# A gated cross-attention and FFN block on Trainium2: the first slots of a software pipeline written out as an opening with its own order, context and Wk/Wv first

## The chip, the cores and the metric

The kernel runs on one core of one Trainium2 chip. Time is device microseconds (us) of one execution, over several executions; the profile is of one execution, taken by the hardware profiler.

## What is computed

A batch `x` of 16 sequences of 256 rows by 512, a context of 16 x 256 x 128. The reference, cut to what matters:

```python
def xattn(q, latent_kv, Wq, Wkv_expand, Wout):      # 16 heads of 32
    qp = q @ Wq.T
    k, v = jnp.split(latent_kv @ Wkv_expand.T, 2, axis=-1)
    scores = jnp.einsum('bhqd,bhkd->bhqk', heads(qp), heads(k)) / jnp.sqrt(32)
    scores = jnp.where(causal, scores, jnp.finfo(scores.dtype).min)
    return merge(softmax(scores) @ heads(v)) @ Wout.T

def ffn(x, w_gate_up, w_down):                      # int8-like quantise and dequantise of
    gate, up = split(qd(x) @ qd(w_gate_up).T)       # rows of x, the weights and h: qd()
    return qd(silu(gate) * up) @ qd(w_down).T

x = x + jnp.tanh(g_xattn[0]) * xattn(layernorm(x), ctx_512, Wq, Wkv_expand, Wout)
x = x + jnp.tanh(g_ffn[0]) * ffn(layernorm(x), w_gate_up, w_down)
```

## The kernel before

Five engines run programs written by hand, in order, and wait for each other on counting semaphores. TensorE (`pe`) multiplies, VectorE (`dve`), ScalarE (`act`) and GpSimd (`pool`) work on tiles, and SyncE (`sp`) issues nearly all DMAs, in order, from one queue.

The attention half is a software pipeline over the 16 batches. `run` calls `slot(b)` for b from -3 to 13, then an ending, then the FFN tiles. In slot b the probabilities of batch b are made and weighed, batch b+1 is scored for its maxima, batch b+2's queries and keys are made and spread, batch b+3 is normalised and transposed, and the outputs of batch b-1 are finished. A step whose batch is not there (`present`) is left out, so slots -3 to 0 are the same list with holes, and slot 1 is the first without any (but for the steps of batches b-2 and b-3, which are on other engines than TensorE).

The steps of one batch X that the texts speak of, in the order in which they depend on each other:

- `load_rows`, `measure_x`, `rsqrt1`, `norm1`: x is loaded to `xln`, its statistics taken (VectorE), the inverse root (GpSimd), normalised (ScalarE).
- `transposed(X, t)`: TensorE transposes `xln` (L1281). `high_t` and `copy_t` (ScalarE) copy it out of PSUM as `xT_hi` and `both`; `low_t` (GpSimd, L537) makes `xT_lo`, their difference. All large products are made of three such products: high by high, low by high, high by low.
- `split_context` (GpSimd, L496 and L498) makes `c_hi`, `c_lo` of the loaded context `craw`; `keys` (L1331) and `values` (L1354) multiply it with Wk and Wv (`wkv_hi`, `wkv_lo`); `queries` (L1344) multiply xT with Wq, 12 products of 128x256 in each of four groups.
- `high_q`, `split_q` (VectorE, L1028), `high_k`, `copy_k`, `low_k` (GpSimd, L545): the same split for q and k.
- `spread_q_hi`, `..._lo`, `spread_k_hi`, `..._lo` (SyncE, L262): four quarters of DMAs of 128 KB each, which lay q and k out by heads in the tile `heads`. Three groups of 32 rows hold hi and lo; two more rows hold the negated maxima against a constant 1 (the memset of `heads`, L1086).
- `scores` (L1295, L1297): one head's scores; `maxima` (VectorE, L995) takes row maxima; `negate`, `maxima_rows` (L1304), `copy_rows` and `move_rows` (the only DMA that ScalarE issues here) put them into `heads`.
- `score_pair` (L1382, L1384): scores of two heads, transposed; `exps` (ScalarE, L775) the exponentials; `select` and `add_blocks` (GpSimd, L522, L530) mask and add; `weigh` (L1408) multiplies with v and sums.
- `weigh_rows`, `weights`, `move_weights`, `load_weights`: the FFN weights are quantised in pieces, one a slot, beside this.

PSUM has eight banks. Two (0, 1) are for scores, two (2, 3) for score pairs, 4 and 5 for weighing and 6 and 7 for everything else, in turn: a table `WORK` says in which order the steps of a slot use the two, and `work_bank` makes each wait until the one before it in that bank has been copied out.

What is done once (the splits of the weights, the tables, the memsets of `heads`) stands in `if b == FIRST` and `if b == FIRST + 1` inside of `slot`.

## Time and profile before

| | us |
|---|---|
| median of 3 runs (lowest to highest) | 771.4 (769.3 to 772.21) |
| the profiled execution | 771.57 |
| its span, first to last instruction | 769.7 |
| busy: TensorE, VectorE, ScalarE, GpSimd | 717.2, 621.4, 412.9, 580.1 |
| mean granted clock of TensorE | 0.971 |

The span is what the trace covers, and times in the trace count from its start. The granted clock is a share of full speed, so 0.50 is the lower of TensorE's two levels (1.2 GHz) and 1.00 the upper (2.4 GHz).

### The profile page before, as it was taken

The numbers are of one execution on the slowest core, as the hardware profiler recorded it, in microseconds if no ns is written. First come the engines' busy times: TensorE is split into PE (matmuls) and PEld (weight loads), VectorE is DVE, ScalarE is ACT, GpSimd is POOL, SyncE is SP. The second block draws the span as 40 slices with busy tenths as digits, with TensorE's granted clock in tenths as the row PEclk, the third lists the DMA queues.
The fourth block names the chain that finished last, engine by engine and source line by source line (L and its number), as shares of the span: only waits on it lengthen the run. The fifth ranks groups of instructions, "written<-read, shape, count | busy, mean of one in ns | idle before, by whom it ended". The sixth has DMA issues, their size and how long they took to land.

```text
span 769.7 us, 17015 instructions
## 1 busy us (share of the span) xinstructions
PE 717.2 (93%) x5345; PEld 515.8 (67%) x5345; DVE 621.4 (81%) x1894; ACT 412.9 (54%) x657; POOL 580.1 (75%) x766
## 2 busy tenths in 40 slices
PE   2488899999999999999999999999999999999993
PEld 2477788798788888888887886755544444444441
DVE  4644867888879789789789878779999999999982
ACT  5433675775765775765765753455534443443440
POOL 5433776887877977977977965668888888888884
PEclk9676999999999999999999999999999999999998
DMA  7685767869769679779779559974846755665665
GB/s 236 154 221 139 203 174 185 203 193 222 199 174 248 169 197 247 174 198 219 201 201 240 141 138 218 244 186 80 162 119 149 160 129 143 153 148 133 146 145 161
DMA packets 137919, 137.59 MB, mean 179 GB/s; under 512 B 90317, under 2 KB 99815, under 8 KB 137703
## 3 DMA queue, kind: packets, MB, share of 16 engines
q1 hardware_dynamic: 136768, 135.97, 71.5%
q8 instruction: 44, 0.72, 0.4%
q10 hardware_dynamic: 1063, 0.54, 0.4%
q14 instruction: 44, 0.36, 0.2%
HBM read 40.24 MB, written 25.31 MB: 85 GB/s over the span
## 4 chain that ended last, share of the span: by engine, by line
PE 60%; issue 13%; POOL 13%; DVE 6%; DMA 5%; ACT 2%; SPq 1%; POOLq 0%; ACTq 0%; DVEq 0%
PE psum L1344 11%; PE psum L1366 10%; PE psum L1408 9%; POOL hidden L664 5%; PE psum L1626 5%; PE psum L1297 5%; PE psum L1382 4%; PE psum L1295 4%; POOL y L678 4%; PE psum L1354 3%; PE psum L1331 3%; DMA x1b<-x_scratch 2%; DMA heads<-nmT 2%; POOL hq L671 2%; PE psum L1636 2%
## 5 line engine op out<-in xcount | busy, mean ns | idle before, releaser
L995 DVE CUSTOM_DVE_ANT_0 junk<-psum,mask 128x128 f32<-128x128 f32 (+1 forms) x512 | 153.7, 353 | 68.9 <-PE psum L1297 66.7
L1626 PE MATMUL psum<-w1q,xqb 128*128 128x512 bf16 (+1 forms) x768 | 158.1, 361 | 1.2 <-DVE u L1036 1.2
L664 POOL TENSOR_TENSOR hidden<-hidden 128x512 f32<-128x512 f32 (+1 forms) x96 | 112.6, 1188 | 28.9 <-ACT hidden L931 28.6
L775 ACT ACTIVATE prob<-psum 128x768 f32<-128x768 f32 x128 | 103.5, 809 | 52.7 <-PE psum L1384 51.4
L1626 PEld LDWEIGHTS psum<-w1q,xqb 128*128 128x128 bf16 x768 | 74.4, 98 | 80.1 <-DVE u L1036 1.6
L936 ACT ACTIVATE hidden<-hidden,round_bias,hinv 128x1408 f32<-128x1408 f32 x32 | 49.9, 1560 | 113.7 <-DVE hinv L1250 113.7
L522 POOL TENSOR_SCALAR_AFFINE_SELECT prob<-prob 128x512 f32<-128x512 f32 x128 | 81.4, 639 | 32.0 <-ACT prob L775 30.9
L530 POOL TENSOR_TENSOR prob<-prob 128x256 f32<-128x256 f32 x128 | 98.1, 772 | 6.5
L1636 PE MATMUL psum<-w2q,hqT 128*128 128x512 bf16 x352 | 82.6, 385 | 6.2 <-DMA hqT<-hq 6.2
L1344 PE MATMUL psum<-xT_hi,wq_hi 128*128 128x256 f32 x256 | 75.8, 296 | 10.0 <-POOL xT_lo L537 10.0
L1297 PE MATMUL psum<-heads 96*128 96x256 f32 x256 | 78.0, 341 | 0.0
L1344 PE MATMUL psum<-xT_hi,wq_lo 128*128 128x256 f32 x256 | 74.6, 291 | 0.0
L1344 PE MATMUL psum<-xT_lo,wq_hi 128*128 128x256 f32 x256 | 74.4, 291 | 0.0
L1382 PE MATMUL psum<-heads 98*128 98x256 f32 x256 | 69.2, 321 | 4.4 <-DMA heads<-nmT 3.9
L1222 DVE SCALAR_TENSOR_TENSOR hidden<-psum,x_scale,s 128x512 f32<-128x512 f32 (+1 forms) x96 | 67.2, 701 | 6.5 <-PE psum L1626 4.2
L1295 PE MATMUL psum<-heads 96*128 96x128 f32 x256 | 69.3, 271 | 3.3 <-DVE mx L995 2.3
L1636 PEld LDWEIGHTS psum<-w2q,hqT 128*128 128x128 bf16 x352 | 34.7, 99 | 46.8 <-issue 9.7
L1232 DVE TENSOR_TENSOR hidden<-psum,s 128x512 f32<-128x512 f32 (+1 forms) x96 | 61.5, 642 | 5.3 <-PE psum L1626 0.2
L1295 PEld LDWEIGHTS psum<-heads 96*128 96x128 f32 x256 | 49.8, 195 | 19.0 <-DVE mx L995 13.7
L1344 PEld LDWEIGHTS psum<-xT_hi,wq_hi 128*128 128x128 f32 x256 | 51.2, 200 | 12.6 <-issue 11.4
L1384 PE MATMUL psum<-heads 98*128 98x128 f32 x256 | 57.4, 224 | 0.0
L931 ACT ACTIVATE hidden<-hidden 128x512 f32<-128x512 f32 (+1 forms) x96 | 50.4, 580 | 11.0 <-DVE hidden L1222 10.9
(116 smaller groups left out, 1798.5 us busy)
## 6 DMA issues: line engine op xcount, KB each, us to landing
heads<-q_hi SPq DMA_DIRECT2D x128, 128.0 KB, 4.3
heads<-k_hi SPq DMA_DIRECT2D x128, 128.0 KB, 4.4
xln<-x_dram SPq DMA_DIRECT2D x16, 512.0 KB, 5.4
heads<-q_lo SPq DMA_DIRECT2D x64, 128.0 KB, 4.0
heads<-k_lo SPq DMA_DIRECT2D x64, 128.0 KB, 3.6
x<-x_dram SPq DMA_DIRECT2D x16, 512.0 KB, 4.2
x_scratch<-x SPq DMA_DIRECT2D x16, 512.0 KB, 4.0
x1b<-x_scratch SPq DMA_DIRECT2D x32, 256.0 KB, 3.4
```

The lines of the kernel that those rows point to most:

```text
L522: pool.affine_select(out=blk, in_=blk, compare_op=ALU.is_ge, fill=0.0, base=0, pattern=[[0, 4], [1, P]], channel_multiplier=-1).then_inc(s ...
L530: pool.tensor_tensor(blk[:, 3], blk[:, 1], blk[:, 2], ALU.add).then_inc(s["added"], 1)
L664: pool.tensor_tensor(up[t % 3][:, o], gate[t % 3][:, o], up[t % 3][:, o], ALU.mult).then_inc(f["prod_done"], 1)
L775: act.activation(prob[:, g % 2, pair % 2, 0:CAUSAL // P].rearrange("p k h q -> p h k q"), psum[:, 2:4, 0:CAUSAL].rearrange("p h (k q) -> p ...
L995: dve.tensor_tensor_reduce(junk[:, n % 2, 0:w], psum[:, h % 2, cols], m, 1.0, LOWEST, ALU.add, ALU.max, mx[:, X % 2, t, h:h + 1]).then_inc ...
L1295: pe.matmul(psum[:, h % 2, 0:P], qs[0:K, X % 2, h, 0:P], ks[0:K, X % 2, h, 0:P], start=True, stop=True)
L1297: pe.matmul(psum[:, h % 2, P:CAUSAL], qs[0:K, X % 2, h, P:S], ks[0:K, X % 2, h, 0:S], start=True, stop=True).then_inc(s["s_done"], 1)
L1344: last = pe.matmul(acc, w[:, k, o], xx[:, k, :], start=(k == n == 0), stop=(k == KH - 1 and n == 2))
L1366: last = pe.matmul(psum[:, bank, :], oo[:, g, o], w[:, g, :], start=(g == n == 0), stop=(g == GROUPS - 1 and n == 2))
L1382: pe.matmul(early, ks[0:K, X % 2, h, 0:P], qs[0:K, X % 2, h, 0:S].rearrange("p (k q) -> p k q", q=P), start=True, stop=True)
L1626: last = pe.matmul(psum[:, bank, 0:w], xqb[:, t % 4, k, :], w1q[:, k, half * I + o:half * I + o + w], start=(k == 0), stop=(k == KH - 1))
L1636: last = pe.matmul(psum[:, 6 + t % 2, :], hqT[:, t % 4, j, :], w2q[:, j, :], start=(j == 0), stop=(j == IT - 1))
```

## The change

`slot(b)` now runs from b = 1, and the steps of slots -3 to 0 are written out in a new function `opening` on each engine, in an order of its own. The same steps are called, each as often as before. SyncE loads the context and Wk/Wv before Wq; Wk/Wv is split first, and the keys and values of batch 0 are multiplied ahead of its queries, in banks 2 to 5, which nothing uses yet. In the opening `work_bank` does not wait; the waits for banks stand in the list itself. The tables of GpSimd are made in two pieces, and the two memsets of `heads` and the tanh of the gates stand at other places.

```diff
-        FIRST = -3
         def work_bank(pe, X, what, t):
 
             at = [w[:2] for w in WORK].index((what, t))
             slot = X - WORK[at][2]
-            if slot >= B - 2:
-                return BANK[what, t]
-            while slot >= FIRST:
+            if slot <= 0 or slot >= B - 2:
+                return bank_of(X, what, t)
+            while True:
...
+        def bank_of(X, what, t):
+
+            first = {("K", 0): 2, ("K", 1): 3, ("V", 0): 4, ("V", 1): 5}
+            return first[what, t] if X == 0 and what in "KV" else BANK[what, t]
...
-        def run(slot, ending, tile):
-
-            for b in range(FIRST, B - 2):
+        def run(opening, slot, ending, tile):
+
+            opening()
+            for b in range(1, B - 2):
                 slot(b)
...
                 sp.dma_start(xln[:], x_tok[0]).then_inc(s["x_loaded"], DMA)
+                sp.dma_start(craw[:], c_bat[0]).then_inc(s["c_loaded"], DMA)
+                sp.dma_start(wkv_raw, WkvT).then_inc(s["wkv_in"], DMA)
                 sp.dma_start(wq_raw, WqT.rearrange("(k p) n -> p k n", p=P)).then_inc(s["wq_in"], DMA)
-                sp.dma_start(wkv_raw, WkvT).then_inc(s["wkv_in"], DMA)
-                sp.dma_start(craw[:], c_bat[0]).then_inc(s["c_loaded"], DMA)
...
+                def opening():
+                    load_rows(1)
+                    spread_k_hi(0, 0)
...
+                def opening():
+                    rsqrt1(0)
+                    split_context(0)
+                    low_t(0, 0)
+                    low_t(0, 1)
+                    low_k(0, 0)
+                    low_k(0, 1)
+                    rsqrt1(1)
...
+                    weights(2)
+                    rsqrt1(3)
+                    split_context(2)
+                    select(0, 0)
...
+                def opening():
+                    high_weights("wkv", wkv_hi, wkv_raw, 1)
+                    norm1(0, 0)
+                    norm1(0, 1)
+                    high_weights("wq", wq_hi, wq_raw, 1)
...
+                    exps(0, 2)
+                    high_k(2, 0)
+                    exps(0, 3)
...
+                def opening():
+                    measure_x(0)
+                    low_weights(0, wkv_hi, wkv_lo, wkv_raw)
+                    low_weights(1, wq_hi, wq_lo, wq_raw)
+                    weigh_rows(0)
+                    measure_x(1)
+                    ones(1)
+                    split_q(0, 0)
+                    split_q(0, 1)
+                    ones(0)
+                    weigh_rows(1)
+                    for h in range(0, 4):
+                        maxima(0, h)
...
+                def opening():
+                    transposed(0, 0)
+                    transposed(0, 1)
+                    keys(0, 0)
+                    keys(0, 1)
+                    values(0, 0)
+                    values(0, 1)
+                    pe.wait_ge(s["t_copied"], 1)
+                    queries(0, 0)
...
+                    pe.wait_ge(s["q_lo"], 1)
+                    transposed(1, 0)
+                    pe.wait_ge(s["q_lo"], 2)
+                    transposed(1, 1)
+                    pe.wait_ge(s["t_copied"], 3)
+                    queries(1, 0)
+                    scores(0, 0)
+                    scores(0, 1)
+                    queries(1, 1)
+                    scores(0, 2)
...
+                    pe.wait_ge(s["t_copied"], 6)
+                    values(1, 0)
+                    maxima_rows(0)
+                    pe.wait_ge(s["t_copied"], 5)
+                    queries(2, 0)
+                    queries(2, 1)
+                    pe.wait_ge(s["v_copied"], 3)
+                    queries(2, 2)
+                    queries(2, 3)
+                    score_pair(0, 0)
+                    pe.wait_ge(s["q_lo"], 5)
+                    values(1, 1)
+                    scores(1, 0)
```

What this does to the engines' programs, at three places. First TensorE's, from its first instruction on. Before, the transposes of batch 0 (`xln`) are followed by the query products (`wq`):

```order
L1281 MATMUL psum<-ident,xln 128x128 x8
L1344 MATMUL psum<-xT_hi,wq_hi 128x256
L1344 MATMUL psum<-xT_hi,wq_lo 128x256
L1344 MATMUL psum<-xT_lo,wq_hi 128x256
L1344 MATMUL psum<-xT_hi,wq_hi 128x256
L1344 MATMUL psum<-xT_hi,wq_lo 128x256
```

Now keys (`wkv`, left out after the first three of twelve) and values (128x512) stand between, and the queries come after them:

```order
L1491 MATMUL psum<-ident,xln 128x128 x8
L1541 MATMUL psum<-c_hi,wkv_hi 128x256
L1541 MATMUL psum<-c_hi,wkv_lo 128x256
L1541 MATMUL psum<-c_lo,wkv_hi 128x256
...
L1564 MATMUL psum<-wkv_hi,c_hi 128x512
L1564 MATMUL psum<-wkv_hi,c_lo 128x512
L1564 MATMUL psum<-wkv_lo,c_hi 128x512
...
L1554 MATMUL psum<-xT_hi,wq_hi 128x256
L1554 MATMUL psum<-xT_hi,wq_lo 128x256
L1554 MATMUL psum<-xT_lo,wq_hi 128x256
```

The 18 products of context and Wk/Wv have moved ahead of the 48 of the queries.

Second, VectorE's program from the first weight split on. Before:

```order
L953 TENSOR_TENSOR wq_lo<-v,wq_hi 128x2048
L1068 TENSOR_REDUCE wmax<-wrow 128x1
L1070 TENSOR_SCALAR w_scale<-wmax 128x1
L1073 RECIPROCAL winv<-w_scale 128x1
L953 TENSOR_TENSOR wkv_lo<-prob,wkv_hi 128x1024
L1086 MEMSET heads 2x4096 x2
L1028 TENSOR_TENSOR q_lo<-psum,q_hi 128x512
L959 BN_STATS st<-xln 128x6 x2
L963 BN_AGGR mv<-st 128x2 x2
L1028 TENSOR_TENSOR q_lo<-psum,q_hi 128x512
L953 TENSOR_TENSOR wo_lo<-prob,wo_hi 128x2048
```

And now (the ISA row is the first of batch 0's maxima; two rows of the weight piece before it are left out):

```order
L1131 TENSOR_TENSOR wkv_lo<-prob,wkv_hi 128x1024
L1131 TENSOR_TENSOR wq_lo<-v,wq_hi 128x2048
L1254 TENSOR_REDUCE wmax<-wrow 128x1
L1256 TENSOR_SCALAR w_scale<-wmax 128x1
L1259 RECIPROCAL winv<-w_scale 128x1
L1145 BN_STATS st<-xln 128x6 x2
L1149 BN_AGGR mv<-st 128x2 x2
L1134 MEMSET heads 2x4096
L1214 TENSOR_TENSOR q_lo<-psum,q_hi 128x512 x2
L1134 MEMSET heads 2x4096
L1254 TENSOR_REDUCE wmax<-wrow 128x1
...
L1181 ISA junk,mx<-psum,mask 128x128
```

Wk/Wv is split first, only one of the memsets of `heads` stands ahead of `q_lo`, `x` of batch 1 is measured before both, and batch 0's maxima follow at once; the split of Wout (`wo_lo`) has left this place.

Third, SyncE's queue of DMAs, the first loads and then what follows them. Before:

```order
L309 DMA xln<-x_dram 128x2x512
L310 DMA v<-WqT_dram 128x4x512
L311 DMA prob<-WkvT_dram 128x1024
L312 DMA craw<-ctxT_dram 128x256
...
L359 DMA xln<-x_dram 128x2x512
L328 DMA craw<-ctxT_dram 128x256
L279 DMA wrow<-w_dram 128x1408
L335 DMA w_scratch<-wint 128x1408
L262 DMA heads<-q_hi 32x1024 x8
L262 DMA heads<-q_lo 32x1024 x4
L359 DMA xln<-x_dram 128x2x512
L262 DMA heads<-k_hi 32x1024 x8
```

And now:

```order
L314 DMA xln<-x_dram 128x2x512
L315 DMA craw<-ctxT_dram 128x256
L316 DMA prob<-WkvT_dram 128x1024
L317 DMA v<-WqT_dram 128x4x512
...
L364 DMA xln<-x_dram 128x2x512
L267 DMA heads<-k_hi 32x1024 x6
L267 DMA heads<-k_lo 32x1024 x3
L284 DMA wrow<-w_dram 128x1408
L333 DMA craw<-ctxT_dram 128x256
L340 DMA w_scratch<-wint 128x1408
L267 DMA heads<-q_hi 32x1024 x2
L267 DMA heads<-q_lo 32x1024
```

The keys of batch 0 are spread before its queries, and before the second weight piece is asked for; q is spread quarter by quarter, high and low in turn.

## Rows read from the trace of the kernel before

**Rows 1.** Windows; after the stretch and its length: engines, PEclk, DMA share, GB/s

```profile
0.00:70.59 70.59, 41.52 (x209) 36.23 (x209) 35.99 (x99) 28.91 (x41) 30.11 (x76) 0.76 0.74 196
70.59:98.49 27.90, 23.81 (x239) 19.60 (x237) 18.68 (x79) 17.41 (x28) 19.41 (x27) 1.00 0.72 179
...
126.50:700.00 573.50, 567.56 (x4385) 410.46 (x4384) 495.38 (x1551) 326.87 (x530) 458.58 (x593) 1.00 0.74 180
```

**Rows 2.** TensorE's timeline: start, us, instruction, [idle before it, releaser]

```profile
15.91 0.55 PE L1344 MATMUL psum<-xT_hi,wq_hi 128*128 128x256 f32 x1 [5.20 <-POOL xT_lo L537]
...
19.02 0.27 PE L1344 MATMUL psum<-xT_lo,wq_hi 128*128 128x256 f32 x1
...
22.96 0.28 PE L1344 MATMUL psum<-xT_lo,wq_hi 128*128 128x256 f32 x1
...
39.17 0.55 PE L1344 MATMUL psum<-xT_hi,wq_hi 128*128 128x256 f32 x1 [3.15 <-POOL xT_lo L537]
...
59.85 0.48 PE L1295 MATMUL psum<-heads 96*128 96x128 f32 x1 [0.31 <-DVE mx L995]
...
61.38 0.48 PE L1295 MATMUL psum<-heads 96*128 96x128 f32 x1 [0.18 <-DVE mx L995]
...
92.30 0.39 PE L1304 MATMUL psum<-ident,nm 128*32 128x128 f32 x2 [1.66 <-DVE nm L1004]
...
98.49 0.39 PE L1382 MATMUL psum<-heads 98*128 98x256 f32 x1 [1.52 <-DMA heads<-nmT]
```

**Rows 3.** VectorE's timeline, 17 to 91 us

```profile
17.80 3.47 DVE L1086 MEMSET heads<- 2x4096 f32 x1 [0.91 <-issue]
...
25.58 0.69 DVE L1028 TENSOR_TENSOR q_lo<-psum,q_hi 128x512 fp32r<-128x512 f32 x1
...
49.64 0.29 DVE L995 CUSTOM_DVE_ANT_0 junk<-psum,mask 128x128 f32<-128x128 f32 x1 [2.81 <-PE psum L1297]
...
50.20 0.29 DVE L995 CUSTOM_DVE_ANT_0 junk<-psum,mask 128x128 f32<-128x128 f32 x1
...
77.75 0.29 DVE L995 CUSTOM_DVE_ANT_0 junk<-psum,mask 128x128 f32<-128x128 f32 x1 [3.94 <-PE psum L1297]
...
90.91 1.10 DVE L1002 TENSOR_SCALAR nm<-mx 128x32 fp32r<-128x32 f32 x1
```

**Rows 4.** ScalarE's timeline, the split of Wq

```profile
9.24 1.89 ACT L693 ACTIVATE wq_hi<-v 128x2048 fp32r<-128x2048 f32 x1
```

**Rows 5.** GpSimd's timeline, xT_lo of batch 0, then slot 0

```profile
12.25 3.56 POOL L537 TENSOR_TENSOR xT_lo<-both,xT_hi 128x512 fp32r<-128x512 f32 x2 [1.54 <-ACT both L724]
...
72.28 0.64 POOL L522 TENSOR_SCALAR_AFFINE_SELECT prob<-prob 128x512 f32<-128x512 f32 x1 [3.20 <-ACT prob L775]
...
74.47 0.41 POOL L496 TENSOR_SCALAR c_hi<-craw 128x256 fp32r<-128x256 f32 x1
...
75.64 1.43 POOL L530 TENSOR_TENSOR prob<-prob 128x256 f32<-128x256 f32 x2
77.16 0.19 POOL L485 TENSOR_SCALAR ve<-mv 128x2 f32<-128x2 f32 x1
...
78.64 0.64 POOL L522 TENSOR_SCALAR_AFFINE_SELECT prob<-prob 128x512 f32<-128x512 f32 x1
...
90.72 2.66 POOL L537 TENSOR_TENSOR xT_lo<-both,xT_hi 128x512 fp32r<-128x512 f32 x2
```

**Rows 6.** The page, DMA issues: count, KB, median us from issue to landing

```profile
heads<-q_hi SPq DMA_DIRECT2D x128, 128.0 KB, 4.3
...
xln<-x_dram SPq DMA_DIRECT2D x16, 512.0 KB, 5.4
```

**Rows 7.** SyncE's timeline, the first eight spreads of q_hi

```profile
23.90 5.05 SPq L262 DMA_DIRECT2D heads<-q_hi  x8
```

**Rows 8.** Windows with the granted clock at 0.50

```profile
26.00:42.70 16.70, 9.03 (x36) 7.71 (x37) 6.75 (x12) 6.96 (x11) 9.52 (x9) 0.50 0.70 169
53.00:70.20 17.20, 14.07 (x58) 12.01 (x58) 9.24 (x51) 5.99 (x10) 6.45 (x5) 0.50 0.77 184
```

More of the change, by code:

```diff
@@ L444, in tile @@
                     store_out(t - 4)
-                run(slot, ending, tile)
+                run(opening, slot, ending, tile)
                 for p in range(2):
@@ L565, in slot @@
                     rsqrt1(b + 3)
-                    if b == FIRST:
-                        tables()
                     select(b, 2)
@@ L685, in tile @@
                     add_residual(t - 4)
-                run(slot, ending, tile)
+                run(opening, slot, ending, tile)
             @block.scalar
@@ L943, in tile @@
                     silu(t, 2)
-                run(slot, ending, tile)
+                run(opening, slot, ending, tile)
             @block.vector
@@ L953, in low_weights, with ones, spread_rows @@
                     dve.tensor_tensor(lo[:], raw, hi[:].bitcast(F32), ALU.subtract).then_inc(s["split"], 1)
+                def ones(half):
+                    dve.memset(ks[3 * HD:3 * HD + 2, half, :, :].bitcast(F32), 1.0).then_inc(s["ones_set"], 1)
+                def spread_rows():
+                    dve.wait_ge(s["sel"], 6)
+                    dve.tensor_copy(spread[:].rearrange("p g c -> p (g c)"), spread_f).then_inc(s["table"], 1)
+                    dve.tensor_reduce(lo_rows[:], lo_tab[:], AX.X, ALU.add).then_inc(s["table"], 1)
                 def measure_x(X):
@@ L1073, in weigh_rows @@
                         dve.reciprocal(winv[:, 0:n], kept).then_inc(s["w_inv"], 1)
+                def opening():
[11 more added lines that the diff above has]
+                        maxima(0, h)
+                    measure_x(2)
+                    maxima(0, 4)
+                    maxima(0, 5)
+                    split_q(1, 0)
+                    maxima(0, 6)
+                    split_q(1, 1)
+                    for h in range(7, 16):
+                        maxima(0, h)
+                    negate(0)
+                    weigh_rows(2)
+                    low_weights(2, wo_hi, wo_lo, wo_raw)
+                    measure_x(3)
+                    spread_rows()
+                    split_q(2, 0)
+                    maxima(1, 0)
+                    split_q(2, 1)
+                    for h in range(1, 16):
+                        maxima(1, h)
+                    negate(1)
+                    weigh_rows(3)
+                    reciprocals(0)
+                    split_reciprocals(0)
                 def slot(b):
@@ L1080, in slot @@
                     measure_x(b + 3)
-                    if b == FIRST:
-                        low_weights(0, wq_hi, wq_lo, wq_raw)
-                        weigh_rows(0)
-                        low_weights(1, wkv_hi, wkv_lo, wkv_raw)
-                        for par in range(2):
-                            dve.memset(ks[3 * HD:3 * HD + 2, par, :, :].bitcast(F32), 1.0).then_inc(s["ones_set"], 1)
                     low_o(b - 1, 0)
@@ L1090, in slot @@
                     split_q(b + 2, 1)
-                    if b == FIRST + 1:
-                        low_weights(2, wo_hi, wo_lo, wo_raw)
-                        dve.wait_ge(s["sel"], 6)
-                        dve.tensor_copy(spread[:].rearrange("p g c -> p (g c)"), spread_f).then_inc(s["table"], 1)
-                        dve.tensor_reduce(lo_rows[:], lo_tab[:], AX.X, ALU.add).then_inc(s["table"], 1)
                     for h in range(2, 6):
@@ L1268, in tile @@
                     up_part(t, 2, 5)
-                run(slot, ending, tile)
+                run(opening, slot, ending, tile)
             @block.tensor
@@ L1648, in tile @@
                     down(t - 3)
-                run(slot, ending, tile)
+                run(opening, slot, ending, tile)
 def kernel(x, ctx_512, g_xattn, g_ffn, L0_xattn_Wq, L0_xattn_Wkv_expand, L0_xattn_Wout, L0_ffn_w_gate_up,
```

249 lines of the change are left out of this document (231 added, 18 removed).

## The prediction

> **What bounds the kernel now.** First the windows [rows 1]. TensorE has hardly an idle moment in the long middle (567.56 of 573.50 us busy) at a granted clock of 1.00, and the change leaves that stretch alone. Before it, TensorE is busy 41.52 of 70.59 us, at a mean clock of 0.76, and 23.81 of 27.90 in slot 0. So the opening waits, and what the first full slot (slot 1, which starts at 98.49) gains passes on to the end one for one: every later slot does the same work in the same order.
>
> Next TensorE's timeline of the opening [rows 2]: idle for 5.20 before the first query product and 3.15 before batch 1's, and the first full slot late by a wait for the DMA of the negated maxima. VectorE's [rows 3] has the first head only at 49.64 and says why: q_lo of batch 0 ends at 26.27 although the queries were done at 23.2, because two memsets of `heads` (17.80 to 25.58, 3.47 each and some 0.9 idle ahead of each) stand before it. The order does the rest: batch 0's scores stand behind all of batch 1's queries.
>
> **The change part by part.** No instruction is added or taken away; places in the queues move, and the waits with them. I play the new order through with the durations of these rows.
>
> *Loads and weight splits, to 21.8.* ScalarE splits Wq from 9.24 on [rows 4]. Now 0.64 MB (context, Wk/Wv) come ahead of Wq's 1 MB. They cost Wq nothing at best and 3.3 us at the mean 196 GB/s of the first 70 us [rows 1]. I take 0.3, since ScalarE does the normalising up to 9.24 anyway. Splitting Wk/Wv lies in ScalarE's wait for x's statistics. Behind Wq's split come the copied transposes and xT_lo on GpSimd (from 12.25, 3.56 for both [rows 5]); that ended at 15.81 and now ends at 16.1. TensorE fills its 5.20 idle us with keys and values of batch 0. The 15 products up to the one at 19.02 came 0.21 apart (0.35 behind the first), the 33 after it, to 22.96, 0.12 apart: the two levels of the clock. Keys are 12 of these, values 6 of double width: 5.1 us at the lower level, hidden. The clock should be up by then, so 48 query products take 5.8: done at 21.8 for 23.2. 1.4 earlier.
>
> *Batch 1's queries, from 39.17 to 27.6.* x of batch 1 is requested after the transposes, near 11 as before, takes 5.4 [rows 6], and some more behind the other first loads; I take 17. VectorE measures it by 18.6, sets one memset to 22.9 and splits q by 24.3; the second memset follows to 28.6. GpSimd has k_lo (1.27 each) by 19.0 and the inverse root (77.16 to 78.64, 1.5) by 20.5, so x is normalised in time. The transposes wait for these two q splits and end at 25.4, copied by 26.4, xT_lo by 27.6. 11.6 earlier. Late next is VectorE: behind its second memset stands the weight piece, about 2, so batch 0's maxima can begin at 30.9.
>
> *Batch 0's heads, end from about 63 to 46.6.* k is spread from 14.9 and q from 23.4, each issue 0.63 (5.05 for eight [rows 7]), 4.3 from issue to landing at the median [rows 6]: the first quarter is there near 30. TensorE comes to the first head at 27.6 + 12 x 0.213 = 30.2. VectorE has 16 heads at 0.56 (49.64 to 50.20), one batch of x (1.5) and two q splits (1.3): 11.8, to 42.7, and waits for queries between heads add some 2: 44.6. Then the clock: while TensorE worked at VectorE's pace before, it stood at 0.50 from 53 to 70.2 [rows 8], and two heads took 1.53 there (59.85 to 61.38) for 1.12. I expect that again from about 40: 8 heads by 0.2, keys and transposes slower too, 2.0.
>
> *Batch 2's queries, the first score pair from 70.59 to 56.0.* Behind the last head come values of batch 1 (1.3), the transposed maxima (0.6) and 48 query products, 19 of them in the first 4 us, 29 in 3.5: 46.6 + 9.4. The maxima's own DMA takes 6.2 from transpose to user (92.30 to 98.49) and is hidden. 14.6 earlier.
>
> *Slot 0, from 27.9 to 23.6.* It has lost three pieces of TensorE's work (one values product, two query groups, 3.6). GpSimd ends last: before it ran from 72.28 to 93.38 (90.72 + 2.66) nearly without a pause, 21.1. Now the split of batch 2's context (74.47 to 75.64, 1.2) waits for a values product, 1.0 into the slot, with the first select behind it; the root (1.5) stands ahead. 56.0 + 1.0 + 1.2 + (21.1 - 1.2 - 1.5) = 76.6, and two query groups (2.9) make 79.5. The second maxima DMA: heads from 57.2, 13.2 for all (77.75 to 90.91), 0.9 for the negation and transposes, 6.2: 77.5, hidden by 2. New on ScalarE: k_hi of batch 2 may be written only once the spreads of batch 1's k have landed, now issued until 54.5; exponentials 3 to 7 are queued behind it. With 4.3 they land at 58.8 and are wanted at 59: nothing, and 1 us for each us later.
>
> *Hidden.* GpSimd's tables, the ones, the spread table and the tanh keep their length and lie in waits; without those, some 3 us in all. Transfers: a share of 0.74 over 98.49 us [rows 1] is 72.9 us of full use, which must fit into 79.5. Close, but it fits, and the last spreads may still land in slot 1, as before.
>
> **Sum.** 98.49 - 79.5 = 19.0. The profiled execution took 771.57 (span 769.7; median of the runs 771.4): 752.6, on the median 752.4; I say 752.5.
>
> The bounds are the clock's. If it does not fall after 31, the 2.0, some 3 us of the slow products behind, and 1 of hops go: 746. If all of slot 0 runs at 0.50, its work (23.81 busy less 3.6, counted dense 18 to 20) takes 1.77 times as long, 32 to 36, and ends at 88 to 92: 761 to 765.
>
> What the clock cost before: 23.10 us of busy time in windows at 0.50 [rows 8], 13.0 at 0.12 for 0.213, so 10.1 us or 1.3% of the span. The Trainium skill ("TensorE: Matmul & The Clock Gate", Part 1) has the default state throttled, with activity releasing it, and the ramp's penalty under 1% of a typical kernel's span. [...]
>
> **Rivals.**
> - *All hides better*, 746: the clock holds through batch 0's heads. In slot 0 it held before, with pauses; in the same kind of work at 53 it fell. 0.17.
> - *The clock stays low through slot 0*, 763. For it: less query work in the slot; against: 48 dense products just ahead. 0.14.
> - *Transfers bind*, 760. If batch 1's k lands 8 us late, ScalarE stands at k_hi and all of slot 0 with it. For it, the 72.9 of 79.5; against, that late quarters only delay heads that VectorE paces. 0.10.
> - *No change*, 770 to 773: it is given back in the middle, where TensorE waits for nothing. 0.03.
> - *Slower*, 780: the clock at 0.50 from the first waits to slot 1. Each us of full-rate work that moves to the low level costs 0.77 (0.213 over 0.12), so the gain is gone when 24.7 us more of it are there. The opening holds 65.3 - 10.1 = 55 us (41.52 + 23.81 busy); all low that is 98, and 9 before the start: slot 1 at 107. Against it, the six dense query groups in the first 31 us. 0.02.
> - The forecast, 0.54, own range 748 to 757.
>
> Range for 8 in 10: 745 to 764. Faster by over 0.5% (3.9 us, about what a measurement of this kernel tells from none) 0.95, same 0.03, slower 0.02.
>
> **What would show it.** In the profile after: keys and values ahead of a first query product near 16; batch 1's queries near 27.6; first head near 30; first score pair at 54 to 58; slot 1 at 77 to 82 with GpSimd's xT_lo as the last wait, and 29 us a slot from there. Wrong would be: ScalarE held at k_hi by spreads for several us, heads held by a quarter that has not landed, 0.50 after 60, or new idle time on TensorE in the middle.

## The result, and the profile after

The changed kernel takes 758.75 us (median of 4 executions, 757.38 to 763.32), the kernel before 771.81 beside it (769.3 to 772.78): a ratio of 0.9846, 95% interval 0.9813 to 0.9879. It is 13 us faster; 19 were forecast, and the range of 745 to 764 holds it. The profiled execution took 758.76, its span is 756.8 and the mean granted clock 0.984.

The milestones, each the start in the trace of an instruction that the prediction named:

| | before | forecast | after |
|---|---|---|---|
| first product of batch 0's queries | 15.91 | 16.1 | 16.81 |
| x of batch 1 measured (VectorE) | 26.19 | 17 | 19.13 |
| first product of batch 1's queries | 39.17 | 27.6 | 30.39 |
| first head's maxima | 49.64 | 30.9 | 33.88 |
| last head's maxima transposed | 63.36 | 48 | 49.77 |
| first score pair (slot 0) | 70.59 | 56.0 | 57.24 |
| first score pair of slot 1 | 98.49 | 79.5 | 82.14 |

So at 57.24 the kernel was 1.2 behind the forecast, and at 82.14 it was 2.6; the rest of the 6.2 us by which 758.75 misses 752.5, about 3.5, was lost behind the start of slot 1. The windows, with the columns of [rows 1]: the opening to the first score pair, slot 0, the middle, then three stretches for the clock and one just before slot 1.

```profile
0.00:57.24 57.24, 38.01 (x236) 34.70 (x237) 38.74 (x104) 30.07 (x42) 30.32 (x80) 0.88 0.90 244
57.24:82.14 24.90, 20.30 (x211) 16.42 (x209) 15.71 (x73) 15.48 (x26) 17.93 (x23) 1.00 0.86 201
110.15:683.65 573.50, 565.25 (x4359) 410.62 (x4377) 494.38 (x1548) 324.41 (x526) 455.99 (x592) 1.00 0.73 180
...
26.00:34.00 8.00, 5.18 (x25) 4.63 (x25) 5.93 (x6) 3.25 (x5) 3.84 (x36) 0.52 1.01 278
...
38.00:50.00 12.00, 10.18 (x68) 8.15 (x66) 11.61 (x59) 7.52 (x13) 7.73 (x10) 1.00 0.88 230
50.00:54.00 4.00, 4.00 (x23) 4.00 (x22) 3.93 (x5) 2.42 (x3) 0.00 (x0) 0.57 1.08 288
...
79.10:82.00 2.90, 0.04 (x1) 0.00 (x0) 0.00 (x0) 0.00 (x0) 0.00 (x0) 1.00 1.02 206
```

Against [rows 1] the DMA engines' share has gone from 0.74 to 0.90 before the first score pair, and from 0.72 to 0.86 in slot 0. In the last row no engine does anything, for three microseconds, while the DMA engines are at 1.02. That is new. TensorE's timeline says who is waited for:

```profile
11.25 0.56 PE L1541 MATMUL psum<-c_hi,wkv_hi 128*128 128x256 f32 x1
...
16.81 0.36 PE L1554 MATMUL psum<-xT_hi,wq_hi 128*128 128x256 f32 x1 [1.85 <-issue]
25.86 1.71 PE L1491 MATMUL psum<-ident,xln 128*128 128x128 f32 x8 [3.07 <-DVE q_lo L1214]
30.39 0.55 PE L1554 MATMUL psum<-xT_hi,wq_hi 128*128 128x256 f32 x1 [2.82 <-POOL xT_lo L606]
...
74.70 0.64 PE L1618 MATMUL psum<-prob,one_in 128*32 128x256 f32 x8 [1.43 <-POOL prob L599]
82.14 0.39 PE L1592 MATMUL psum<-heads 98*128 98x256 f32 x1 [3.00 <-DMA heads<-nmT]
84.84 0.39 PE L1592 MATMUL psum<-heads 98*128 98x256 f32 x1 [0.81 <-ACT prob L891]
```

Keys and values (11.25 to 14.96, 3.7 us) fill most of what was an idle stretch of 5.20 [rows 2]. What ends the 1.85 idle before the first query product is not named there; GpSimd's xT_lo ends at 16.71. Slot 1 waits for the DMA of the negated maxima, as before, but for 3.00 and no longer 1.52. ScalarE's timeline around it:

```profile
73.71 1.19 ACTq L912 DMA_DIRECT2D heads<-nmT  x2
74.95 1.56 ACT L813 ACTIVATE wrow<-wrow,round_bias,winv 128x1408 f32<-128x1408 f32 x1 [1.27 <-DVE winv L1259]
83.49 0.60 ACT L862 ACTIVATE q_hi<-psum 128x512 fp32r<-128x512 f32 x1 [6.98 <-DMA heads<-q_lo]
83.99 0.81 ACT L891 ACTIVATE prob<-psum 128x768 f32<-128x768 f32 x1
```

The maxima's DMA is issued at 73.71 and used at 82.14, 8.4 us for 5.4 before (its issue there is at 93.1), and ScalarE is held for 6.98 by the spreads of batch 2's q. It is free only at 83.49, and the exponentials that stand behind `high_q` come 1.35 after slot 1 has begun. SyncE's timeline (issues) shows what both are queued with:

```profile
69.04 1.14 SPq L267 DMA_DIRECT2D heads<-k_hi  x2
70.23 1.35 SPq L267 DMA_DIRECT2D heads<-q_lo  x2
71.62 1.49 SPq L267 DMA_DIRECT2D heads<-q_hi  x2
73.15 0.58 SPq L364 DMA_DIRECT2D xln<-x_dram  x1
73.84 0.51 SPq L267 DMA_DIRECT2D heads<-k_lo  x1
74.39 1.44 SPq L267 DMA_DIRECT2D heads<-q_hi  x2
75.87 0.59 SPq L267 DMA_DIRECT2D heads<-q_lo  x1
```

The last spread of q is issued at 75.87, behind three k's and the 512 KB of batch 4's x; ScalarE waits for it until 83.49.

VectorE, with [rows 3] for comparison: x of batch 1 comes late, and the rest of the order is as forecast.

```profile
19.13 1.29 DVE L1145 BATCH_NORM_STATS2 st<-xln 128x6 f32<-128x512 f32 x2 [2.86 <-DMA xln<-x_dram]
...
21.61 3.47 DVE L1134 MEMSET heads<- 2x4096 f32 x1 [0.91 <-issue]
25.11 1.29 DVE L1214 TENSOR_TENSOR q_lo<-psum,q_hi 128x512 fp32r<-128x512 f32 x2
27.31 3.47 DVE L1134 MEMSET heads<- 2x4096 f32 x1 [0.91 <-issue]
...
48.20 1.29 DVE L1188 TENSOR_SCALAR nm<-mx 128x32 fp32r<-128x32 f32 x1
```

Of the 16.3 us gained at slot 1, 12.9 are left in the span. The product that spreads the reciprocals marks each slot on TensorE's timeline; before it stood at 99.00, 128.10 and 450.32:

```profile
82.66 0.57 PE L1528 MATMUL psum<-rec,spread 128*128 128x256 f32 x3
...
112.87 0.69 PE L1528 MATMUL psum<-rec,spread 128*128 128x256 f32 x4
...
377.97 0.39 PE L1592 MATMUL psum<-heads 98*128 98x256 f32 x1 [1.15 <-DMA heads<-nmT]
...
437.26 0.69 PE L1528 MATMUL psum<-rec,spread 128*128 128x256 f32 x4
```

The lead is 16.3 at slot 1, 15.2 at slot 2 and 13.1 at slot 13. Slot 1 gives back 1.1 (30.21 for 29.10). Of the other 2.1, waits like the one at 377.97 explain 0.9: the kernel before has one of them there (0.91 at 216.14), this one two (1.15, and 0.70 at 201.22). The rest lies in slots of 29.4 us in place of 29.1 to 29.2 without a wait over 0.25, and I have not traced it.

### The profile page after: what moved, and what is told of

Read it like the earlier page. It is cut to its first block, busy times and chain, and to the rows that moved or that the text cites. A ratio compares the mean times of both kernels' runs of the same rounds, so it can differ in the third digit from the quotient of the medians.

```text
span 756.8 us, 16991 instructions
## 1 busy us (share of the span) xinstructions
PE 710.4 (94%) x5321; PEld 511.7 (68%) x5345; DVE 622.6 (82%) x1894; ACT 413.2 (55%) x657; POOL 578.7 (76%) x766
## 3 DMA queue, kind: packets, MB, share of 16 engines
q1 hardware_dynamic: 136768, 135.97, 72.3%
## 4 chain that ended last, share of the span: by engine, by line
PE 58%; issue 12%; POOL 11%; DMA 8%; DVE 5%; SPq 4%; ACT 1%; POOLq 0%; ACTq 0%; DVEq 0%
PE psum L1554 10%; PE psum L1576 9%; PE psum L1618 9%; PE psum L1507 5%; PE psum L1935 5%; POOL hidden L776 5%; PE psum L1592 4%; PE psum L1505 4%; POOL y L790 3%; PE psum L1541 3%; DMA x1b<-x_scratch 3%; PE psum L1564 3%; POOL hq L783 2%; PE psum L1945 2%; DMA heads<-nmT 2%
## 5 line engine op out<-in xcount | busy, mean ns | idle before, releaser
L1945 PE MATMUL psum<-w2q,hqT 128*128 128x512 bf16 x341 | 80.7, 385 | 6.7 <-DMA hqT<-hq 6.2
L1592 PEld LDWEIGHTS psum<-heads 98*128 98x128 f32 x256 | 48.7, 190 | 12.3 <-DMA heads<-nmT 7.4
```

The costliest lines, as they stand in the source:

```text
L1592: pe.matmul(early, ks[0:K, X % 2, h, 0:P], qs[0:K, X % 2, h, 0:S].rearrange("p (k q) -> p k q", q=P), start=True, stop=True)
L1945: last = pe.matmul(psum[:, 6 + t % 2, :], hqT[:, t % 4, j, :], w2q[:, j, :], start=(j == 0), stop=(j == IT - 1))
```

## The experiments

**Theory T**, from the trace after: the opening is now so short that batch 2's spreads bind at its end, at two places: the maxima's small DMA lands late among them, and `high_q` of batch 3 waits for q. **Rivals**: the 3 us idle is a chance of this execution; or the missing 6 us are elsewhere (ScalarE's order, the clock). Behind each time stand, in brackets, its ratio to the kernel before, measured beside it, and the 95% interval of the ratio. The length of slot 1 is always that between two marks of the kind above. Each trace is of one execution, and executions of one kernel differ by some microseconds, in the time of a milestone too: batch 1's queries start at 30.39 in the changed kernel and at 32.19 in its repeat.

**A repeat of the changed kernel, unchanged.**

> The changed kernel as it is, again, for a tighter interval and for what varies from run to run. It took 758.75 (757.4 to 763.3). In its trace the first full slot starts at 82.14 after 3.00 us of wait for the DMA of the maxima; from the broadcast of slot 1 to that of slot 13 it needs 2.4 us more than the kernel before, 1.1 of it in slot 1. Theory T (the transfers of the opening are crowded, and two of its last DMAs land late): the 3.00 and the 1.1 come again within 1 us, as they have one cause each time; the later 1.3 comes and goes. Rival V (chance delays of one run): the 3.00 us or the wait of ScalarE for the q spreads is not there. Time 757 to 761 by both.

758.61 us (0.9822, 0.9792 to 0.9853). Slot 1 at 82.58 after 3.34 for the maxima's DMA, ScalarE held 7.91 by q_lo, slot 1 takes 30.80. Both waits repeat; they are no chance. The first maxima's DMA is not quite hidden here either: slot 0 starts at 57.28 after 0.29 of wait for it, and in nine of the ten kernels below that have the new opening after 0.67 to 4.05.

**q ahead of k in SyncE's tail.** Bytes and count of the DMAs are the same:

```diff
+                    spread_q_lo(2, 1)
+                    load_weights(3)
                     spread_k_hi(2, 0)
-                    load_weights(3)
+                    load_context(3)
                     spread_k_hi(2, 1)
-                    load_context(3)
+                    spread_q_hi(2, 2)
+                    spread_q_lo(2, 2)
+                    spread_q_hi(2, 3)
+                    spread_q_lo(2, 3)
                     spread_k_hi(2, 2)
-                    spread_q_lo(2, 1)
-                    spread_q_lo(2, 2)
-                    spread_q_hi(2, 2)
                     load_rows(4)
                     spread_k_lo(2, 0)
-                    spread_q_hi(2, 3)
-                    spread_q_lo(2, 3)
                     spread_k_lo(2, 1)
```

> In SyncE's opening the spreads of batch 2's q go ahead of most of its k; nothing else moves and the bytes are the same. Theory T: ScalarE's wait for the q spreads at the head of slot 1 (6.98 us, to 83.49) ends at about 78 to 80, and slot 1 takes 29.2 us again for 30.2; the DMA of the maxima still lands late, as the same bytes are in flight, so slot 1 starts at 81 to 82.5. Time 757.5, 1.1 less than the changed kernel. Rival G (GpSimd and TensorE end last anyway, and the lost time is of the middle): no change beyond 0.5 us. Rival K (k of batch 2 is now late): TensorE waits at a head of batch 2 in slot 1 and the time grows by 1 to 3 us.

755.76 (0.9786, 0.9755 to 0.9816), 2.9 less than the repeat. ScalarE's wait is gone and slot 1 takes 29.14, both as theory T had it. The maxima's DMA ends 0.83 after its user could start (81.08): it took 6.3 from issue to use, for 8.4 and 8.8 (repeat), with the same bytes in flight. Theory T had it late still, with slot 1 at 81 to 82.5; slot 1 is at 81.08 although slot 0 began 1.0 later than in the repeat. So the DMA's lateness hangs on the order and not on the bytes alone.

**Exponentials ahead of `high_q` in slot 1**: ScalarE does `exps(1, 0)` before `high_q(3, 0)`, SyncE stays as it was.

> In ScalarE's slot 1, and only there, the exponentials of the first pair go ahead of the copy of q that waits for batch 2's q spreads. DMAs are unchanged. Theory T: the wait at the head of slot 1 no longer holds the exponentials; the second pair comes 1.7 us after the first as in the kernel before (98.49, 100.22), where it now comes 2.7 after; 1.0 us less, 757.6. Rival G: slot 1 takes 30.2 us still, as something else is late behind it (q_lo of batch 3): no change.

759.07 (0.9826, 0.9796 to 0.9856): no gain. ScalarE waits for no DMA and the second pair comes 1.8 behind the first, as theory T said, and still slot 1 takes 30.91. The windows of this kernel, behind 3.08 idle before 80.94:

```profile
80.94:82.94 2.00, 2.00 (x13) 1.84 (x14) 0.00 (x0) 1.29 (x3) 0.40 (x1) 0.92 0.47 113
82.94:84.00 1.06, 0.90 (x5) 0.72 (x5) 0.92 (x2) 1.06 (x4) 0.24 (x1) 0.50 0.03 12
84.00:86.00 2.00, 2.00 (x7) 1.72 (x8) 2.00 (x4) 1.04 (x2) 0.99 (x2) 0.50 0.04 8
```

For about three us the clock stood at its lower level, which costs about what the wait saved. That was in no expectation: the idle time for the small DMA has a second price, in most executions. In the changed kernel and its repeat the clock stayed at 1.00 behind 3.00 and 3.34 idle; in six of the traces of this section it is at or near 0.50 within some us of the start of slot 1.

**One more 512 KB load** (of x, into a tile that nothing reads there) behind batch 4's x. It adds a transfer and changes nothing that is computed.

> One more DMA of 512 KB (a tile of x, loaded a second time, not used) behind the load of batch 4's x in SyncE's opening, in the stretch of 70 to 82 us in which the DMA share is 1.0. Theory T: the DMA of the maxima, issued at about 73.7, and the q spreads behind it land later by what those bytes take, 512 KB at the 220 to 270 GB/s there, 1.9 to 2.3 us, plus 0.6 of issue: slot 1 starts at 84 to 85 and the time is 2 to 3 us more, 761.3. Rival G: GpSimd's xT_lo and the queries (to 78.9) bind with the 3.00 as chance: under 0.7 us.

761.87 (0.9862, 0.9828 to 0.9897), 3.3 more. ScalarE's timeline, TensorE's, and a window:

```profile
87.18 0.60 ACT L865 ACTIVATE q_hi<-psum 128x512 fp32r<-128x512 f32 x1 [8.52 <-DMA heads<-q_lo]
```

```profile
83.17 0.39 PE L1595 MATMUL psum<-heads 98*128 98x256 f32 x1 [1.86 <-DMA heads<-nmT]
...
88.53 0.58 PE L1595 MATMUL psum<-heads 98*128 98x256 f32 x1 [3.47 <-ACT prob L894]
```

```profile
88.00:92.00 4.00, 3.47 (x14) 3.18 (x15) 3.81 (x8) 2.58 (x5) 2.07 (x3) 0.57 0.00 1
```

The total is what theory T gave (761.3), but only one of its two places is borne out. Slot 0 had begun 2.1 later than in the repeat, before the added load, so times count from there: ScalarE gets q's tile 27.8 us into it, for 26.2 and 27.2 (repeat), and the second pair comes 5.4 behind the first, for 2.7 and 3.3. So the added bytes delay the spreads of q, by 0.6 to 1.6. The maxima's DMA is not late by them: slot 1 starts at 83.17 and not at 84 to 85, after a shorter wait (1.86), though the load was asked for at 76.34, 0.45 behind that DMA (75.89), which took 7.3. The pause of 3.47 was then followed by the lower clock, a part of this kernel's loss, and slot 1 took 34.3.

**The tail in order of need**: as the kernel with q ahead, and the loads of weights 3 and context 3 moved ahead, x of batch 4 last.

> SyncE's opening once more: batch 2's q ahead of most of its k, and besides the weight piece and the context are asked for some 7 us earlier, in a pause of the queue, and x of batch 4 last, so that 1.2 MB stand outside of the crowded stretch of 70 to 82 us. With q first alone, slot 1 started at 81.1 after 0.83 of wait. Theory T (the DMAs of the maxima and of q are late behind those bytes): the DMA of the maxima lands 1 to 2 us sooner, slot 1 starts at 79.5 to 80.3, bound by GpSimd's xT_lo and batch 3's queries; slot 1 takes 29.2. Time 754.5, about 1 under q first. Rival S (SyncE's own issue, 0.6 a DMA and as many of them, sets when the last spreads land): slot 1 at 81 as with q first, no change against it.

754.01 (0.9771, 0.9741 to 0.9801). Slot 1 starts at 79.36, with no wait over 0.25 for the maxima's DMA, and takes 29.16. The time is 4.6 us below the repeat; against q ahead alone (755.76) the 1.8 us are not told from the spread of either. Slot 1 starts where the forecast had put it (79.5) and behind the work it had named, but by two errors that cancel: batch 1's queries start at 31.20 for 27.6, and slot 0 takes 21.8 for 23.6. As three things move at once (x, the weights and context, q), which of them frees the maxima's DMA is not shown.

**Wout's load behind batch 1's x**, with the tail in order of need:

```diff
-                for g in range(GROUPS):
-                    sp.dma_start(wo_raw[HD * g:HD * (g + 1), :, :],
...
                     load_rows(1)
+                    for g in range(GROUPS):
+                        sp.dma_start(wo_raw[HD * g:HD * (g + 1), :, :],
...
```

> As the run before, and the four loads of Wout (1 MB) stand behind the load of batch 1's x. In the changed kernel that x landed at 19.10, 7.5 us after its issue, where I had 17. Theory T (the first loads' bytes in the queue make it late, and VectorE with it): x lands 2 to 3 us sooner, VectorE's memset and q splits, the transposes and batch 1's queries follow 2 us sooner (28.4 for 30.4 in the trace of the changed kernel), and so does slot 1: 752.5. Rival Q: VectorE waits for the q that ScalarE copies (normalised x stands ahead of it there), so only 0.5 to 1 us comes through; or the split of Wout on ScalarE waits for its load and holds batch 1's normalising: no gain.

752.84 (0.975, 0.9721 to 0.9779), 1.2 below the kernel it is built on, which the spread of the runs does not tell from none. x is measured at 16.27, with no wait for it; in the eight traces with x's load behind Wout's and the context first it was 18.34 to 20.82, always with one. The queries of batch 1 start at 29.04, 2.2 earlier than with Wout's load ahead (31.20); VectorE's gain was 3.3, and the rest goes since ScalarE now splits Wout from 20.66 on, ahead of the normalising. Slot 1 starts at 77.38 and takes 29.1. (The profiled execution took 750.08, 2.8 under the median.)

**And Wout's split behind batch 1's transposes**, on ScalarE.

> As the run with Wout's loads later, and ScalarE's split of Wout (1.9 us) goes from ahead of batch 1's normalising to behind the copies of its transposes. In the trace of that run it waited for its load until 20.66 and held x and q_hi until 22.48 and 23.18. Theory T: q_hi at 22.1, q_lo bound by VectorE's memset (22.2): 22.9 and 23.6 for 24.48 and 25.7, batch 1's queries at 27.8 for 29.04 and slot 1 1.2 us earlier at 76; 751.6. Rival: the weight piece and the split now stand ahead of high_q of batch 1 on ScalarE and its wait for the q spreads (5.07 us, to 38.75) hides it; that wait ends with the spreads, which come no earlier: no change.

751.55 (0.9761, 0.9733 to 0.9788), not to be told from the one before. Queries of batch 1 at 28.55, slot 1 at 78.24. ScalarE's copy of them waits until 39.73, 6.54 of it for the spreads of batch 0's q: the half microsecond won ahead of the spreads is lost in them. Slot 1 was expected at 76; it comes later than in the trace before, as the rival said.

**The parts of the change, one undone at a time.** First both memsets ahead of the splits of q:

```diff
                     ones(1)
+                    ones(0)
                     split_q(0, 0)
                     split_q(0, 1)
-                    ones(0)
```

> The changed kernel with one part undone: both memsets of heads stand ahead of batch 0's q splits on VectorE, as before, not one of them. By the chain of the prediction the splits, the transposes of batch 1 and its queries come 3.47 + 0.9 = 4.4 us later, and nothing of it is made up, as VectorE's maxima follow the queries' heads: first head 37.5 for 33.1; slot 1 later by 3.5 to 4.4; 762.5. Rival C (VectorE's total binds and the order within is free, since the memset has to be paid anyway before the maxima): first maxima at 37.5 for 33.9 at most, but the wait for transfers behind takes part of it: 1 to 2 us only, 760.

763.60 (0.9901, 0.9868 to 0.9934), 5.0 more than the repeat. TensorE waits 8.94 for q_lo, batch 1's queries start at 36.58 and slot 1 at 87.02. In the repeat, whose x of batch 1 landed at about the same time (20.50, here 20.63), these are 32.19 and 82.58: 4.4 each, which is the price that the prediction's chain gives, and nothing of it is made up.

**Batch 0's heads behind batch 1's queries**, as before the change, and not between them.

> The changed kernel with another part undone: batch 0's first heads stand behind all four of batch 1's query groups, not between them. The first head then comes at 30.4 + 4.6 to 6.9 for 33.1, so at 36 to 37. By the chain of the prediction VectorE's 16 heads start 3 us later and end 2 to 3 later: 761. Rival C: VectorE had waits for queries between heads anyway (1.06, 1.90), which vanish, so the last head comes 0 to 1 us later: 759.

764.57 (0.992, 0.9888 to 0.9953), 6.0 more, where theory T had 2.2. First maxima at 40.11 (35.68 in the repeat), and the clock is at 0.60 from 42 to 48, where the heads go at VectorE's pace; in the changed kernel and its repeat it was 1.00 there. It is near 0.50 from 88 to 94 too, behind 3.38 of wait for the maxima's DMA. This trace is of the slowest of the five executions (768.68), so its lengths are not those of the median.

**The memsets alone, in the kernel before**, moved behind the first splits of q.

> The kernel before with one part of the change alone: both memsets of heads go from ahead of batch 0's q splits to behind the spread table, where VectorE was idle for 11.8 us. By my reading of the trace of before (q_lo ends at 26.27 because of them): q_lo at 21.1 and 24.0, keys at 23.3 for 26.33, batch 1's transposes and queries 3 to 5 us earlier (34.5 to 36 for 39.17), slot 1 as much: 767. Rival O (the order of the queues, not the memsets, sets the stretch: batch 1's copies wait for k_lo, its x for ScalarE): 1 us or less, 770.5.

766.95 (0.9951, 0.9928 to 0.9973), 3.9 less than the kernel before beside it (770.88): what theory T gave, 767. The trace does not show where the gain lies, as it is of the second longest of the ten executions (770.90). TensorE's timeline of this kernel:

```profile
33.92 0.55 PE L1344 MATMUL psum<-xT_hi,wq_hi 128*128 128x256 f32 x1 [3.44 <-POOL xT_lo L537]
43.10 0.79 PE L1354 MATMUL psum<-wkv_hi,c_hi 128*128 128x512 f32 x1 [3.25 <-DVE q_lo L1028]
...
62.68 0.61 PE L1304 MATMUL psum<-ident,nm 128*32 128x128 f32 x2 [0.33 <-DVE nm L1004]
```

And ScalarE's:

```profile
40.18 1.56 ACT L701 ACTIVATE wrow<-wrow,round_bias,winv 128x1408 f32<-128x1408 f32 x1 [7.99 <-DVE winv L1073]
41.65 0.58 ACT L746 ACTIVATE q_hi<-psum 128x512 fp32r<-128x512 f32 x1
```

The queries of batch 1 are 5.25 earlier than in [rows 2], the transposed maxima 0.7. The second memset now ends at 38.1 and holds VectorE's weight piece, ScalarE waits 7.99 for its scale (`winv`), and the copy of q stands behind that. So in this execution the 5 us won at the queries are lost again, and slot 1 starts at 98.26 for 98.49: the wait goes on to another piece of the old order. What the shorter executions did otherwise (seven of the ten have a mean clock of 0.98, this one 0.973) has no trace.

**Context, Wk and Wv behind the queries again**: the loads, splits and products of context 0 in the old order, in the new opening.

> The changed kernel with the context's part undone: loads in the old order, Wq split first, and batch 0's keys and values behind its queries, with the spreads of q ahead of those of k to match. By the chain of the prediction the 5.1 us of products no longer lie in TensorE's wait for xT_lo. Theory T: queries of batch 0 end at 23 to 24 for 22.8, keys and values follow (2.9 to 5.1 us), k_lo ends some 9 us later than 20.0, the copies of batch 1's transposes and its queries behind it: 33.5 to 35 for 30.4, the first head at 37 to 38 for 33.1; slot 1 and the time 3 to 5 us later, 763. Rival C: VectorE's memsets and batch 1's x bound this stretch anyway, so only 1 us is lost, 760.

776.89 (1.0081, 1.005 to 1.0111): 18 us more than the repeat of the changed kernel, where 3 to 5 were expected, and slower than the kernel before. The trace shows a fault of this kernel's order, not only of the part undone. SyncE issues nothing from 11 to 32.64, since the first weight piece, which it waits for, and batch 1's inverse root stand on GpSimd behind `low_k(0, ...)`, which now came at 27.19. The first head runs at 45.35. So one more kernel frees these two queues: root and piece ahead of k_lo, and batch 1's normalising between the copies of q.

> e8_context_behind took 776.9 because two queues stood behind k_lo of batch 0, which now came only at 29.7: on GpSimd batch 1's inverse root and the first weight piece (32.6), on SyncE, which waited for that piece from 10.96 to 32.64, all spreads of q, whose tile was ready at 25. This kernel moves the root and the piece ahead of k_lo on GpSimd, and ScalarE's normalising of batch 1 between the copies of q; batch 0's keys and values stay behind its queries. Theory A (the 18 us are these two queues; the place of the context's products itself is worth only k_lo's delay): q spreads from about 22, first head at 36 to 38 for 33 in the changed kernel, slot 1 at 83 to 86, 757 to 762. Theory B (the place of the keys itself costs the 18 us, because the heads need k): first head still at 45, slot 1 above 95, over 770.

768.15 (0.9948, 0.9924 to 0.9972). Its tail is that of the changed kernel, so its measure is the repeat (758.61): 9.5 us more. Slot 1 starts at 91.78, and neither theory is right. The first head starts at 35.22, only 0.3 later than in the repeat (34.89), so theory B is wrong, and the 8.7 us between this kernel and the one before it (776.89) are those two queues; but 9.5 are left, where theory A had at most 3.4. Windows of the kernel with q ahead, whose queue is that of the changed kernel up to 63 us, and then of this one:

```profile
0.00:20.00 20.00, 8.85 (x53) 8.31 (x54) 6.96 (x10) 12.33 (x16) 11.04 (x21) 1.00 0.93 260
20.00:30.00 10.00, 4.68 (x31) 4.08 (x29) 7.67 (x8) 5.22 (x9) 3.11 (x6) 0.85 0.58 160
30.00:40.00 10.00, 7.87 (x48) 7.90 (x48) 7.04 (x22) 1.95 (x2) 5.80 (x39) 0.64 1.05 265
40.00:50.00 10.00, 9.11 (x58) 7.15 (x56) 9.64 (x54) 7.51 (x13) 7.06 (x10) 1.00 0.89 252
```

```profile
0.00:20.00 20.00, 6.08 (x27) 5.74 (x28) 8.79 (x14) 10.96 (x11) 8.63 (x19) 1.00 0.78 226
...
40.00:50.00 10.00, 8.00 (x49) 7.07 (x47) 6.70 (x35) 4.11 (x8) 4.09 (x8) 0.83 1.00 281
50.00:60.00 10.00, 8.47 (x48) 7.25 (x48) 8.65 (x28) 5.11 (x8) 4.60 (x4) 0.83 1.02 209
60.00:70.00 10.00, 7.72 (x46) 7.24 (x45) 5.06 (x20) 3.90 (x6) 4.94 (x11) 0.78 0.64 147
```

With the context first, k's six high spreads are issued at 14.88. In this kernel they come after q from 29.02 on; the 34 GB/s less in the first 20 us (19 less than the 245 of the repeat) are 0.4 to 0.7 MB, of the 0.8 that these six are. SyncE asks for batch 2's x behind them, at 37.37 and not 31.37; VectorE waits 1.99 for it in the midst of batch 0's heads (42.10), the maxima are transposed at 54.79 for 50.84 in the repeat, and their DMA takes 9.1 for 5.6. Slot 0 starts at 64.69 for 57.28 in the repeat, 7.4 later. Then the clock: 0.50 from 66 to 70 (1.00 in the other two). Slot 0 takes 27.1 for 25.3, slot 1 32.6 for 30.8. 7.4 + 1.8 + 1.8 is 11.0, of the 12.3 between the two spans (this trace's execution took 770.35, 2.2 over its median). So 9.5 us is the price of this order as a whole, the late x of batch 2 in it; the place of the products alone is not separated from it.

The parts, undone singly, cost 5.0, 6.0 and 9.5 us, 20.5 together for a gain of 13: they are not additive. My reading is that each one's delay runs into the same spreads and the same low clock; no run tests it.

## Why the prediction was partly right

The direction, the mechanism and most of its places were right; of the sum of 19.0, 16.3 came at slot 1, and 12.9 were left at the end. By its own steps:

- *Loads and splits, to 21.8.* Queries of batch 0 start 0.7 later than forecast: Wq is split at 10.13, 0.9 later than in [rows 4], and not for its load, which is where the forecast's 0.3 stood, but for GpSimd. Its last small step of the root took 1.00, and 0.19 before (7.59), while VectorE split Wk/Wv. GpSimd's row, VectorE's, and GpSimd's in the kernel with context, Wk and Wv behind and the two queues freed, where VectorE splits Wk/Wv only at 15.25:

```profile
7.67 1.00 POOL L559 TENSOR_TENSOR nb<-nb,rs 128x2 f32<-128x2 f32 x1
```

```profile
7.39 1.23 DVE L1131 TENSOR_TENSOR wkv_lo<-prob,wkv_hi 128x1024 fp32r<-128x1024 f32 x1 [1.14 <-ACT wkv_hi L805]
```

```profile
7.54 0.20 POOL L559 TENSOR_TENSOR nb<-nb,rs 128x2 f32<-128x2 f32 x1
```

It took 0.99 to 1.06 in all ten traces with that split beside it, and 0.19 to 0.20 in the four without. The split that was moved into an idle stretch thus had a price on the path, by its neighbour. TensorE was at full speed before the queries, as forecast: its products are 0.21 apart up to 12.68 and 0.12 from there. (The granted clock in the windows reads 1.00 over both stretches, and so it does before, where 15 products up to 19.02 go 0.21 apart; the spacing decides. The 10.1 us that the prediction gives for the clock leave out this first stretch.)
- *Batch 1's queries, 27.6.* They came at 30.39, 2.8 late. The mis-sized term is the landing of x, 2.1 of it: 17 was taken, 19.13 measured. 7.5 us from issue (11.63) to use, for the 5.4 of [rows 6], with Wout's load ahead in the queue. With Wout's load behind it, x was there by 16.27, so that load is the cause.
- *Heads, end at 46.6.* VectorE's maxima began 3.0 late (33.88 for 30.9) and ended 1.6 late, at 48.2: the 2.0 for the clock in these heads did not come, it held 1.00 from 38 to 50. It fell from 50 to 54, in batch 2's queries (0.21 a product for 0.12), which the forecast had too, as 19 products in their first 4 us. In the repeat it did not fall there, and TensorE waited for the first maxima's DMA instead (0.29), which the forecast had as hidden. Where the heads stand behind the queries, as in [rows 8] and in the kernel that puts them back, they do go with a low clock; what differs is query work between them.
- *Slot 0, GpSimd last at 76.6.* GpSimd's last xT_lo ends at 75.9, and the two query groups behind it were done at about 79.1, where 79.5 was forecast. The closeness is partly luck: the slot began 1.2 late, and GpSimd's work behind the context's split, taken at 18.4, needed 16.0 (59.91 to 75.89).
- *The step that failed* stands in two places: "The second maxima DMA: ... 77.5, hidden by 2", and "Close, but it fits, and the last spreads may still land in slot 1, as before". The maxima were transposed at 72.88, 1.6 later than its terms give (71.3), which with its 6.2 would have been 79.1, just hidden; but the DMA took 9.3 from there (8.4 from its issue, not 5.4). It runs while spreads and loads that had 98.49 us before have 82.14 with the same bytes; that their order makes it late is shown (6.3 with q ahead, no wait in order of need), by which of them is not. And what waits in slot 1 for the spreads is not the heads but ScalarE's first instruction, `high_q(3, 0)`, which may write only when batch 2's q has left. Both waits were removed by order alone, and slot 1 then started at 79.36.
- The rival "Transfers bind" (760, 0.10) was nearest to what happened, in time and in kind; its place, `k_hi`, was wrong, and what it priced, a k 8 us late, did not occur. It was argued from a mean share over the whole opening, 72.9 of 79.5 (slot 0's own share was 0.72, which makes it 72.3); what decided was the last 12 us of it, at a share of 1.04.
- *The clock holds, or stays low in slot 0*: it was 1.00 from 54 on, so neither price of these rivals was paid in the changed kernel.
- *The middle, one for one.* A lead of 15.2 at slot 2 was 13.1 at slot 13. From slot 1 to 13 it is 351.3 before, 354.6 after, 353.3 in the repeat and 350.8 with Wout later, each in one execution; 1.1 and 1.7 of it are slot 1's, by ScalarE's wait, and for the rest I did not find a cause in the change. The about 3.5 us behind the start of slot 1 are more than half of the 6.2 by which the forecast missed, and "one for one" is the step that had them at nothing.

What stays open: whether the low clock behind 2 to 3.5 us of idle time follows a rule here, since it fell in six traces and not in two others; which transfers make the maxima's DMA late; and what the middle's 2 us hang on.

## What to carry to other kernels

When an opening gets shorter, its bytes do not: add up what must be transferred between the first load and each wait, put the transfers in order of who is waiting, and look at each engine's first instruction behind the shortened part. Work that needs little input, moved ahead, lets its transfers start early too; here that seems to be the larger part (3.7 us of products filled TensorE's idle time, and putting them back cost 9.5, with a late x in it). An experiment that undoes one part of a hand-written order must move every queue that the part was threaded through, or it measures a stall of its own. And a kernel that undoes one part is measured against the kernel that has all the others.

## What the runs showed of the hardware

- A DMA of 2 x 16 KB from ScalarE's queue took 5.4 us from issue to use before, 8.4 and 8.8 (repeat) in the changed kernel, 6.3 with q ahead of k and 7.3 with one more load of 512 KB just behind it, all beside SyncE's spreads of 128 KB and a load of x, which was asked for ahead of it in the first (73.15 for 73.71) and behind it in the repeat (74.14 for 73.82). The Trainium skill ("DMA: Bandwidth & Descriptors", Queues, rings and completion order) has each DMA engine take packets in turn from the queues that have work. By that alone one would expect a small DMA on a queue of its own to pass the other queue's backlog; the rows have times of issue and use only, and do not show whether it did.
- At a full share the DMA engines moved 206 GB/s (79.1 to 82) in one stretch and 288 (50 to 54) in another. I did not take apart what sets this.
- Behind 3.08 us of idle time TensorE ran some 2 us at 1.00 and then 3 at 0.50; behind 3.38 it was low at once (0.50 from 88 to 94), behind 2.85 (work from 87.02, 0.50 from 88 to 90) and 2.63 (work from 91.78, 0.50 from 94 to 98) a little later. Behind 3.00 and 3.34 in the changed kernel and its repeat it stayed at 1.00. The length of the pause alone does not decide it in this range.
- From 11.25 to 12.68 in the changed kernel, and up to 19.02 in the kernel before, products went 0.21 apart while the granted clock of the windows reads 1.00.
- Beside a subtraction of 128x1024 on VectorE (1.23 us) a GpSimd step on 128x2 takes 1.00 us for 0.19, in ten traces of ten. VectorE's own 128x32 step took 1.29 at 48.20, beside GpSimd's xT_lo, and 0.23 at 72.11.
